# Two reorderings in VectorE's queue where an attention stage changes its softmax shift

## The reference

```
K = ctx @ Wk.T + bk ;  V = ctx @ Wv.T + bv
att = Q @ K.T * 512**-0.5 + (b1 + b2 - b3) * phi      # 512 x 8192
w = softmax(att) ;  x = x + w @ V
```

## Time and profile before

| | us |
|---|---|
| median of 3 runs | 705.67 |
| lowest and highest | 704.83, 705.8 |
| the profiled execution, its own time | 705.45 |
| its span | 703.7 |
| TensorE busy in the span | 691.9 |
| VectorE busy in the span | 551.8 |
| ScalarE busy in the span | 337.3 |

### The profile page before, as it was taken

The page is one execution under the profiler, slowest core; times in us unless marked ns, Lnnn a source line. Parts: engine busy times, 40 slices in busy tenths (PEclk is TensorE's granted clock), DMA queues, the critical chain, the costliest instruction groups (busy, mean ns, idle before and its releaser), DMA issues.

```text
span 703.7 us, 9942 instructions
## 1 busy us (share of the span) xinstructions
PE 691.9 (98%) x3237; PEld 571.9 (81%) x3237; DVE 551.8 (78%) x702; ACT 337.3 (48%) x451; POOL 198.5 (28%) x144
## 2 busy tenths in 40 slices
PE   7999999999999999999999999999999999999997
PEld 6888888888887788888888888878888888788885
DVE  6577787888969998899996653769434799899897
ACT  4322222222245555566663333742233588887872
POOL 4345545454440000000000000426784111211245
PEclk9999999999999999999999999999999999999999
DMA  8046677766642236433210701614200889999984
GB/s 310 6 164 213 220 219 243 249 219 234 227 147 90 89 121 249 169 107 102 89 60 1 283 1 68 236 49 169 92 2 2 313 338 344 400 382 381 385 305 150
DMA packets 38686, 130.70 MB, mean 186 GB/s; under 512 B 6658, under 2 KB 10756, under 8 KB 35588
## 3 DMA queue, kind: packets, MB, share of 16 engines
q1 hardware_dynamic: 35828, 124.45, 49.4%
q0 software_dynamic: 1536, 4.20, 1.8%
q10 hardware_dynamic: 1296, 1.71, 0.7%
HBM read 120.89 MB, written 9.46 MB: 185 GB/s over the span
## 4 chain that ended last, share of the span: by engine, by line
PE 84%; DVE 5%; DMA 4%; issue 3%; ACT 2%; POOL 2%; POOLq 0%; DVEq 0%; SPq 0%; ACTq 0%
PE ps L927 22%; PE ps L894 8%; PE ps L890 8%; PE ps L891 8%; PE ps L826 5%; PE ps L828 5%; PE ps L827 5%; PE ps L1110 4%; PE ps L1140 3%; PE ps L1121 2%; PE ps L1119 2%; PE ps L1120 2%; POOL met L488 2%; DMA raw_u<-up_in 1%; PE ps L1045 1%
## 5 line engine op out<-in xcount | busy, mean ns | idle before, releaser
L431 POOL TENSOR_TENSOR c_lo<-ring,c_hi 128x512 fp32r<-128x512 f32 x64 | 86.5, 1351 | 100.5 <-ACT c_hi L548 100.5
L548 ACT ACTIVATE c_hi<-ring 128x512 fp32r<-128x512 f32 x64 | 40.4, 633 | 128.2 <-PE ps L894 93.0
L436 POOL TENSOR_TENSOR w_lo<-raw,w_hi 128x1024 fp32r<-128x1024 f32 x11 | 26.8, 2438 | 261.8 <-ACT w_hi L675 247.2
L890 PE MATMUL ps<-qk_hi,c_hi 128*128 128x512 f32 x256 | 100.2, 391 | 0.1
L891 PE MATMUL ps<-qk_lo,c_hi 128*128 128x512 f32 x256 | 99.6, 389 | 0.0
L1305 DVE TENSOR_TENSOR runmax<-runmax,att 128x512 f32<-128x512 f32 x64 | 87.4, 1366 | 6.0 <-DVE att L1299 3.2
L1614 DVE TENSOR_TENSOR wu_lo<-raw_u,wu_hi 128x2048 fp32r<-128x2048 f32 (+1 forms) x33 | 69.7, 2112 | 15.4 <-ACT wu_hi L685 15.0
L1299 DVE SCALAR_TENSOR_TENSOR att<-ring,beta,ps 128x512 f32 (+1 forms) x64 | 47.8, 747 | 27.4 <-PE ps L894 26.8
L894 PE MATMUL ps<-qk_hi,c_lo 128*128 128x512 f32 x256 | 68.4, 389 | 0.0
L927 PE MATMUL ps<-p_hi,d_hi 128*128 128x512 f32 x256 | 64.2, 393 | 0.6 <-DVE ps L1382 0.6
L927 PE MATMUL ps<-p_hi,d_lo 128*128 128x512 f32 x256 | 63.2, 389 | 0.0
(11 more groups left out here) (305 smaller groups left out, 1472.5 us busy)
## 6 DMA issues: line engine op xcount, KB each, us to landing
ring<-stream SPq DMA_DIRECT2D x64, 512.0 KB, 4.2
raw_u<-up_in SPq DMA_DIRECT2D x22, 1024.0 KB, 7.2
raw_d<-down_in SPq DMA_DIRECT2D x33, 512.0 KB, 7.1
ring<-ctx_in SPq DMA_DIRECT2D x32, 512.0 KB, 3.3
raw<-shared_in SPq DMA_DIRECT2D x11, 768.0 KB, 4.4
raw_u<-up_last_in SPq DMA_DIRECT2D x11, 768.0 KB, 6.8
slots<-blank SPq DMA_DIRECT2D x15, 256.0 KB
late<-wqkv_in SPq DMA_DIRECT2D x1, 3072.0 KB, 10.3
```

Source lines behind the costliest of these rows:

```text
L431: pool.tensor_tensor(c_lo[:, s % 2, :], ring1[:, s, 0, :], c_hi[:, s % 2, :].bitcast(F32), ALU.subtract).then_inc(lo1_ready, 1)
L548: act.activation(c_hi[:, s % 2, :], ring1[:, s, 0, :], ACT.Copy).then_inc(hi1_ready, 1)
L890: pe.matmul(ps[:, s, :], hi, qk_hi[:, k, :], start=(k == 0), stop=False)
```

## The change

VectorE's queue is reordered at two places; no operation is added or taken away, no other engine's program changes.

1. `shift_columns(2, 0, diag_b)` is moved ahead of `early_shift(3)`, the shift of the fourth pair, pair (0, 3).
2. The four multiplications of the banks by `factor`, with the waits in front of them, are moved ahead of `probabilities_low(1, 0)`, the low part of the probabilities of the fifth pair, pair (1, 0).

```diff
             early_shift(2)
             lows(0, 1)
+            shift_columns(2, 0, diag_b)
             early_shift(3)
-            shift_columns(2, 0, diag_b)
             lows(0, 2)
             dve.wait_ge(shift_ready, 2)
             early_shift(4)
...
             lows(0, 3)
             early_shift(5)
             context_low(1, 0)
-            probabilities_low(1, 0)
             dve.wait_ge(factor_ready, 1)
             for d in range(KC):
                 if d < KC - 1:
...
                 else:
                     dve.wait_ge(pv_done, GROUP + 2)
                 dve.tensor_tensor(ps[:, 4 + d, :], ps[:, 4 + d, :], factor[:, :], ALU.mult).then_inc(rescaled, 1)
+            probabilities_low(1, 0)
             dve.wait_ge(summed, GROUP + 2)
```

## The result

| | before | after |
|---|---|---|
| median of 20 runs, us | 706.53 (704.83 to 707.54) | 705.43 (703.73 to 706.66) |
| profiled execution: its own time, span | 705.45, 703.7 | 705.51, 703.8 |

The forecast was 704.5 with 705.67 for the kernel before, a ratio of 0.9984; over more runs the kernel before stands at 706.53, which is why the measured 705.43 lies higher in the range than the gain alone would put it.

The account below looks back on a forecast made before the run. TensorE, busy 98% of the span, bounds the kernel; of its 1.77 us of second-pass pauses, VectorE's reordered queue gives 1.13. 705.67 − 1.13 = 704.54, said 704.5; range 703.6 to 705.6, the forecast's own 704.0 to 705.1.

Parts of the forecast that it names:

- TensorE's two pauses: Second pass: 0.52 us before the spread (L906), waiting on `diag_b`, and 1.25 us at (1, 0); together 1.77 us.
- Edit 1 costs and gains nothing alone: Moving `shift_columns` first: spread starts 0.52 us earlier, but TensorE waits 0.52 longer at (1, 0); rescales still start at 234.35.
- The cover named: ScalarE's queued copy of `shift_b`, ending about 223.7, hides the later `early_shift(3)`, which ends 1.2 us earlier.
- TensorE's wait on the first rescale: At (1, 0) in the second pass, forecast to stay after the change, at 0.1 to 0.2 us.
- Edit 2 gains what it passes: Rescales pass one VectorE instruction, the low part of (1, 0)'s probabilities, and start 1.13 us earlier; gain 1.13, not 1.77.
- The bank's signal: Bank 0 visible to VectorE 0.42 us after its last matmul starts; 0.03 too late if only the rescales are moved.
- What is late next: `d_lo` of (1, 1) is the tightest operand: margin 0.06 us, TensorE's wait taken as 0, kept at 0 to 0.15.
- Through to the end: After the second pass: a transfer sets the pace, but TensorE's progress releases it, so the 1.13 us carries through.
- TensorE's whole pause goes: Rival, chance 0.09: both second-pass pauses vanish, gain 1.77 us, time 703.9.
- The banks seen late: Rival, chance 0.12: banks visible later, or `d_lo` of (1, 1) holds TensorE; rescales only 0.25 us earlier, 705.4.
- No gain at the end: Rival, chance 0.10: gain real at 240 us but lost in the experts' stage, whose pace a transfer sets; 705.7.
- Slower: Rival, chance 0.05: experts' stage met at another phase of its transfers; two more late loads give 707.7.

Follow-up runs that it names:

- one shift moved: Kernel with both changes, plus the third pair's shift, `early_shift(2)`, moved into the first pass: second pass 175.72 us, ratio 0.9968 to the kernel before.
- two moved: Kernel with both changes, plus `early_shift(2)` and `early_shift(3)` moved into the first pass: second pass 175.71 us, ratio 0.9965 to the kernel before.
- edit 2 alone: Kernel after with `early_shift(3)` put back ahead of `shift_columns`, so only the rescales are moved: second pass 176.37 us, ratio 0.9983 to the kernel before.
- the pad ahead: Kernel after plus one extra 0.60 us VectorE operation ahead of the rescales: second pass 176.79 us, one run of 705.72 us.

## Why the prediction was right

**What bounds it.** Right: TensorE's two pauses, and behind 235 us TensorE alone. The 1.14 gained at 241 us (29.31 from the start of the pass to (1, 1), before 30.45) is there at the end of the pass.

**Edit 1 costs and gains nothing alone.** Right in the second pass: 177.33, as before. The copy of `shift_b` on ScalarE started 12.43 us into the pass (224.47), before at 13.05; 0.62 earlier where 0.52 was forecast, since the spread, when it does not wait, also passes 0.1 quicker (223.87 − 223.41 = 0.46, before 223.10 − 222.54 = 0.56). The cover named, ScalarE's queue, held: `p_hi` of (0, 3) came 0.6 earlier, not later. For the same reason TensorE's wait on the first rescale is larger than the 0.1 to 0.2 given: 235.44 − (233.39 + 1.81) = 0.24.

**Edit 2 gains what it passes.** Right: the rescales 1.14 us earlier for 1.13 in the sum, second product of (1, 0) at 25.67 for 25.69 worked out. The Trainium skill, "VectorE: DVE Perf Modes", section "The DRAIN you can't avoid", has the next operation wait for an empty pipe, which was read as 1.22 for the instruction passed. The same section adds that a next operation that is not held starts earlier, and the trace has it so: the operations of this size in front of the rescales start 1.13 to 1.14 apart in every kernel.

**The bank's signal.** Mis-sized. I took 0.42 us from the start of the bank's last matmul, from ScalarE's wait on a whole product; with one shift moved, where VectorE stands idle for it, that matmul starts at 232.62 + 0.23 = 232.85 and the rescale at 233.34, 0.49 later; with two moved and with edit 2 alone it is 0.49 as well. Edit 2 alone therefore waits 0.11 and not 0.03 on the first bank. The remaining 0.07 of the 0.18 are 0.02 in the rescaled product and 0.04 in the one behind it (239.80 − 237.94 = 1.86 for 1.82), which I did not follow up. It changed nothing in the sum for both edits: there bank 0 can be taken at 233.39 + 0.23 + 0.49 = 234.11, 0.49 before the rescales start at 234.60, and about that much, 0.47, is what moving one more shift gave.

**What is late next.** Right in place and in size: `d_lo` of (1, 1), no stall in the kernel after, 0.09 us to spare where 0.06 at the signal and up to 0.15 in the load were given.

**Through to the end.** Right in what arrives, not in the reason. From the end of the second pass to the end of the span it is 315.6 to 315.9 us in each of the ten profiled executions, 315.7 before and 315.6 after, so nothing of the gain is given back there. The prediction had "a transfer sets the pace" there, from the 8.80 us load wait on the chain of before. Such a wait is on the chain in only one of the nine other executions (8.87 us, one shift moved); the chain of after goes through TensorE at that place, and the stage is at most 0.3 us longer in the two with the wait. So the transfer was not a cost that decides the time.

**The level.** The time given, 704.5, rested on three runs at 705.67; twenty have 706.53, and 706.53 − 1.13 = 705.40. One profile could not tell it: the profiled execution of the kernel before opened its first pass earliest of all ten (last section). So the measured 705.43 lies outside the forecast's own 704.0 to 705.1, and inside 703.6 to 705.6, by 0.17, only because that range was widened for the rivals. That the absolute time fell inside is luck; what bears the prediction out is the difference, 1.14 us in the second pass for 1.13.

**The rivals.** "TensorE's whole pause goes" fails because VectorE's queue is the bound: the pad ahead costs all of its 0.60. The banks seen late had 705.4, almost the time measured, but with a gain of 0.25 where the second pass has 1.14; that agreement is one of level alone. No gain at the end is refuted by the length of the stage behind. Slower did not occur.

## What to carry to other kernels

Where two engines hand over to each other, a pause of the busy one is worth what its source's queue gives up, not its own length: 1.77 us of pauses gave 1.14, and one of the two edits nothing by itself, because its pause only moved to the next handover. Follow the late engine's queue back for the last stretch without idle time; work in it that the waiting operation does not need (here a low part, then a shift that fits into another stage's idle time) is the gain, until the next input binds (here the first bank, once one more shift was taken out). Behind a gain of this kind look for the operand that the unchanged queue now delivers with the least to spare.

## What the runs showed of the hardware

I had not expected that the stage ahead of the first pass differs by up to 1.5 us between executions, though no edit touches it, and by 1.3 between two of one program. The first weight load of L890, which opens the first pass, starts between 33.8 and 35.3 us in the ten profiled executions of this study. The timeline of TensorE at its opening, the kernel before:

```profile
3.14 2.93 PE L836 MATMUL ps<-ident,ones 128*128 128x128 f32 x12 [3.14 <-POOL lower L414]
6.89 0.66 PE L810 MATMUL ps<-ident,ln_a 128*128 128x128 f32 x4 [0.82 <-DVE ln_a L1246]
7.38 0.83 PE L836 MATMUL ps<-ident,ones 128*128 128x128 f32 x6
...
11.52 1.04 PE L810 MATMUL ps<-ident,ln_a 128*128 128x128 f32 x8
```

and the same kernel run again:

```profile
3.14 2.93 PE L836 MATMUL ps<-ident,ones 128*128 128x128 f32 x12 [3.14 <-POOL lower L414]
6.95 1.12 PE L810 MATMUL ps<-ident,ln_a 128*128 128x128 f32 x4 [0.88 <-DVE ln_a L1246]
7.85 1.49 PE L836 MATMUL ps<-ident,ones 128*128 128x128 f32 x6
...
12.81 1.03 PE L810 MATMUL ps<-ident,ln_a 128*128 128x128 f32 x8
```

Both open at the slow pace: twelve matmuls in 2.93 us, about 0.24 each. Then the same transposes and matmuls take 0.66 and 0.83 us (0.14 for each matmul of L836) in one execution and 1.12 and 1.49 in the other, and this one is at the quick pace only from about 12 us on. The granted clock of these windows reads 1.00 in both, so the rows do not say that it is the clock; they say that TensorE's pace nearly doubles at a moment that varies, by 6.9 us in one and some 5 us later in the other. By 12.81 against 11.52 the two are 1.29 us apart, and they come to the second pass 1.29 apart, at 210.65 and 211.94: more than the whole change is worth. In each of the nine executions other than the first of the kernel before, the six matmuls of L836 take 1.48 or 1.49 us, and they open the first pass at 34.4 to 35.3 us. Since the first pass is 176.87 to 176.89 us in all ten and the stage behind the second 315.6 to 315.9, the opening is where their spans differ when the second pass does not. A comparison of two spans would have shown this change as nothing.
